# Shorter lag of the state sums, another order in the norm stage and in the first feed-forward tiles

## Chip, cores and metric

The kernel runs on one core of a Trainium2 chip. Time is device microseconds of one execution; the figure that counts is the median of several executions, lower is better.

## What is computed

One decoder layer over x (4 rows of the batch, 512 tokens, 512 wide) and a context ctx (4, 512, 256), all float32: attention, a selective scan gated by x, and a feed-forward part whose weights are drawn from a table of 16 values, each behind a residual and a layer norm.

```python
x = _layernorm(x + attn(x, weight_qkv, weight_proj))
x = _layernorm(x + ssm(ctx_1024, x, ...))      # x is the gate z
x = _layernorm(x + ffn(x, lut, gate_idx, up_idx, down_idx))

# ssm, per batch row: 512 channels, 16 states, 512 steps
x = einsum('ed,bld->bel', in_proj_w, ctx); u = silu(conv(x) + conv_b)
dt_lo, Bm, Cm = split(einsum('ke,bel->bkl', x_proj_w, u))
delta = softplus(einsum('er,brl->bel', dt_proj_w, dt_lo) + dt_proj_b)
state = state * exp(delta_t * A) + (delta_t * u_t) * B_t      # every step t
y = sum_n(state * C_t) + D * u
return y * silu(z)

# ffn
h = silu(x @ lut[gate_idx].T) * (x @ lut[up_idx].T)           # 1376 wide
return h @ lut[down_idx].T
```

## The kernel before

Each engine has a program of its own, written out by hand; its order is the order of the code, and semaphores tie the engines together. Nothing reorders it.

**Ramp (up to about 57 us).** SP loads in order: the table, the weights ip, ctx, xT (four loads), the first chunk of index words, wqkv. VectorE does the convolution's taps (`earlier_taps`, L1125), and behind the first and the second set the two integer operations on the index words (L1336, L1339). ScalarE makes u (`silu_u`, L822). TensorE does the kv projections (L563), which need xT and wqkv, and then the x projection (L577), which needs u.

**Scans (57 to 541 us).** The scan runs in 64 groups g (16 states for each of 4 batch rows), each of ET = 4 units et of 128 channels by 512 steps: 256 units k. For every unit TensorE transposes the scaled input into one of NB = 4 PSUM banks (`input_transposed`, L665), once the scan of unit k - 4 has freed the bank; VectorE scans it (`scan`, L1224); Pool multiplies the state by C (`output_product`, L1524). In the last batch row VectorE does the product of et = 3 itself (L1217, L1221). The states of the groups below G0 = 56 are added up in DRAM by accumulating DMAs of Pool's queue, even and odd groups apart. Those of groups 56 to 63 are added up on TensorE in PSUM (`state_summed`, L677): one pass per unit through the identity, two instructions of the trace. A sum waits for its unit's product and stands behind the input transpose of the unit 12 later. `rest_summed` (L683) adds what the DMAs have summed up for the last row.

**Norm stage (541 to about 612 us).** Batch rows b = 0 to 3, halves k = 0 to 7 (k = 2b and 2b + 1, two tiles of 128 tokens each). ScalarE makes the gates (`gates`, L999, L1000), those of row 3 once x1 of row 3 is loaded into hT, and then the high part of the first weights (`high_part`, L1046). VectorE multiplies y by the gate (`gate_y`, L1272, for row 3 L1269 out of PSUM); TensorE transposes the product (`y_over`, L715); VectorE adds x1 and takes the statistics (`norm_stats`, L1282 to L1292); Pool raises to -1/2 (`stage2_rstd`, L1614); VectorE makes the shift (`norm_shift`, L1297); ScalarE applies both (`norm_apply`, L1006); TensorE transposes (`x2_over`, L727); ScalarE writes the rounded high part (`x2T_hi`, L1017), VectorE the remainder (`x2T_lo`, L1306). TensorE does, for k = 0 to 7, x2_over(k), y_over(k + 3), and from k = 3 on halves of the first gate/up product between them. y_over(4) waits for gate_y(3), which frees its banks, and for its own row's gate_y(2). Pool's order is stage2_rstd(0) to (3), `low_part(0, 0)` (L1629, the remainder of the first weights), stage2_rstd(4) and on.

**Feed-forward (612 to 849 us, then the down product).** Weights are decoded in chunks, gate_up(f) and down(f), from one byte per entry: ScalarE makes 7 leaves (`leaves`, L1036), Pool the eighth (L1624), and VectorE joins them in 7 selects (`select`, L1252), each waiting for certain leaves. After select 2 and 3 VectorE spreads the bits of the next chunk (`then`, L1231, L1236). SECOND is the chunk gate_up 1, decoded while the norm stage runs; WITH_HALF says behind which half ScalarE makes which of its leaves. TensorE does `gate_up(f)` in four blocks tb (L743, 24 matmuls each); ScalarE's `silus` (L1052) and VectorE's `inner` (L1313) turn a block into hT. TensorE's block tb of tile f + 1 waits for inner(f, tb), and all of it for the low part of its weights. In `tile(f)` the decodes of down f and gate_up f + 2 are mixed with the silus and inners; tile(0) stands ahead of the loop over f.

## Time and profile before

| | us |
|---|---|
| median of 3 runs | 983.32 (982.26 to 984.1) |
| profiled execution | 979.72 |
| its span, first to last instruction | 977.9 |

| engine | busy us | share |
|---|---|---|
| TensorE matmul | 843.4 | 86% |
| VectorE | 779.3 | 80% |
| ScalarE | 668.1 | 68% |
| Pool (GpSimd) | 480.1 | 49% |

The mean granted clock of TensorE is 0.918 of full speed. The shares are means over stages with different limits; each stage has to be read for itself. Of an engine's idle time the trace names what ended it. Idle time of an engine that others do not wait for costs nothing.

### The profile page before, as it was taken

To read this page: it belongs to the slowest core of one execution; us is meant where nothing else is said; L and a number is where in the kernel's file an instruction comes from. 1 tells how busy PE (TensorE), PEld (TensorE's weight loads), DVE (VectorE), ACT (ScalarE), POOL (GpSimd) and SP (SyncE) were. 2 spreads that over 40 slices of the span, in tenths; PEclk is the share of its full clock that TensorE was granted. 3 is DMA by queue.
4 is the path that set the end of the run, shared out by engine and by line. 5 is a ranking of instruction groups with operands and counts; after the bars stand their busy time and mean duration, and the time that the engine had idled before them with its cause. 6 is when DMAs were issued, how large, how long until landed. Compare 5 with 4: busy or idle time off the path is not lost.

```text
span 977.9 us, 11750 instructions
## 1 busy us (share of the span) xinstructions
PE 843.4 (86%) x3736; PEld 609.0 (62%) x3736; DVE 779.3 (80%) x1084; ACT 668.1 (68%) x989; POOL 480.1 (49%) x456
## 2 busy tenths in 40 slices
PE   7879897878779697887879858799999999899996
PEld 3547644557445574546555457687777778688885
DVE  5997899887998969987699897888888887355543
ACT  4598995689966899658689346777777776242321
POOL 3169966799866999569877231211121111001000
PEclk9899878989789897798879979899999999999999
DMA  8057988689996799967999722111111110223221
GB/s 289 35 158 177 216 181 211 118 227 238 220 218 137 200 224 223 226 136 171 219 228 306 196 78 100 52 44 43 43 45 62 43 43 22 75 86 108 86 65 54
DMA packets 50340, 137.04 MB, mean 140 GB/s; under 512 B 5540, under 2 KB 13860, under 8 KB 41588
## 3 DMA queue, kind: packets, MB, share of 16 engines
q0 software_dynamic: 8064, 58.72, 31.6%
q1 hardware_dynamic: 40864, 77.49, 23.3%
q8 instruction: 23, 0.38, 0.2%
q10 hardware_dynamic: 1364, 0.25, 0.1%
q14 instruction: 25, 0.20, 0.1%
HBM read 58.46 MB, written 79.04 MB: 141 GB/s over the span
## 4 chain that ended last, share of the span: by engine, by line
issue 21%; PE 18%; DVE 15%; ACT 9%; POOL 5%; DMA 1%; DVEq 1%; ACTq 0%; POOLq 0%
PE banks L768 4%; PE banks L627 4%; DVE leaf L1252 3%; PE banks L743 3%; ACT leaf L1036 2%; DVE w_gu L1252 2%; PE banks L677 2%; POOL state L1524 2%; DVE state L1224 2%; PE banks L665 2%; ACT decay L921 2%; ACT scaled L908 2%; DMA y_scratch<-state 1%; DVE idx_sb L1236 1%; DVE w_down L1252 1%
## 5 line engine op out<-in xcount | busy, mean ns | idle before, releaser
L1524 POOL TENSOR_TENSOR state<-state,crep 128x512 f32<-128x512 f32 x243 | 333.4, 1600 | 80.5 <-DVE state L1224 80.4
L1224 DVE TENSOR_TENSOR_SCAN state<-decay,banks 128x512 f32<-128x512 f32 x243 | 280.8, 1203 | 54.8 <-PE banks L665 44.9
L743 PE MATMUL banks<-x2T,wgu 128*128 128x512 f32 x1056 | 250.1, 396 | 10.0 <-DVE hT L1313 5.4
L665 PE MATMUL banks<-ident,scaled 128*128 128x128 f32 x1024 | 171.1, 308 | 77.0 <-DVE state L1224 56.6
L743 PEld LDWEIGHTS banks<-x2T,wgu 128*128 128x128 f32 x1056 | 199.3, 190 | 58.8 <-DVE hT L1313 13.3
L665 PEld LDWEIGHTS banks<-ident,scaled 128*128 128x128 f32 x1024 | 132.4, 157 | 149.6 <-DVE state L1224 65.5
L921 ACT ACTIVATE decay<-delta,negA 128x512 f32<-128x512 f32 x256 | 170.4, 730 | 75.1 <-DVE state L1224 66.9
L908 ACT ACTIVATE scaled<-duT,BT 128x512 f32<-128x512 f32 x256 | 164.4, 728 | 0.3 <-issue 0.3
L1036 ACT ACTIVATE leaf<-idx_sb,table,table_gap 128x512 f32<-128x512 uint8 (+1 forms) x126 | 122.5, 1014 | 7.1 <-DVE w_down L1252 3.1
L1623 POOL TENSOR_TENSOR pool_wait_here<-minus_half 128x1 f32<-128x1 f32 x21 | 5.2, 246 | 181.7 <-DVE w_gu L1252 116.8
L1252 DVE COPY_PREDICATED leaf<-idx_sb,leaf 128x512 f32<-128x512 uint8 (+1 forms) x84 | 89.0, 1060 | 5.9 <-issue 4.9
L768 PE MATMUL banks<-x2T 128*128 128x512 f32 (+1 forms) x264 | 83.1, 396 | 3.5 <-DVE x2T L1461 3.5
L768 PE MATMUL banks<-x2T,wgu 128*128 128x512 f32 (+1 forms) x264 | 81.5, 390 | 0.0
L1659 POOL TENSOR_TENSOR rstd<-vareps,minus_half 128x1 f32<-128x1 f32 x16 | 8.7, 544 | 140.7 <-DVE vareps L1480 140.7
L627 PE MATMUL banks<-wp,attT 128*128 128x512 f32 x128 | 64.0, 647 | 0.0
L768 PEld LDWEIGHTS banks<-x2T 128*128 128x128 f32 (+1 forms) x264 | 50.6, 192 | 14.7 <-issue 3.9
L1537 POOL DMA_DIRECT2D y_scratch<-state x52 | 56.1, 1079 | 2.4 <-DMA y_scratch<-state 2.4
L768 PEld LDWEIGHTS banks<-x2T,wgu 128*128 128x128 f32 (+1 forms) x264 | 49.6, 188 | 10.4
L1113 ACT ACTIVATE leaf<-leaf,shift,rstd 128x512 f32<-128x512 f32 x16 | 13.1, 817 | 62.6 <-DVE shift L1483 62.6
L1252 DVE COPY_PREDICATED w_gu<-idx_sb,leaf 128x1024 f32<-128x1024 uint8 x30 | 48.5, 1618 | 0.1
L569 PE MATMUL banks<-wqkv,xT_sb 128*128 128x512 f32 x96 | 44.7, 610 | 1.5 <-DVE conv_in L1181 1.5
L1046 ACT ACTIVATE wgu<-w_gu 128x1024 fp32r<-128x1024 f32 x11 | 11.7, 1060 | 50.1 <-DVE w_gu L1252 50.1
(152 smaller groups left out, 1164.4 us busy)
## 6 DMA issues: line engine op xcount, KB each, us to landing
y_scratch<-state POOLq DMA_DIRECT2D x52, 1024.0 KB, 8.9
crep<-c_scratch SPq DMA_DIRECT2D x64, 256.0 KB, 5.8
idx_sb<-in_idx SPq DMA_DIRECT2D x10, 512.0 KB, 3.6
xT_sb<-in_xT SPq DMA_DIRECT2D x16, 256.0 KB, 5.0
y_scratch<-u SPq DMA_DIRECT2D x4, 1024.0 KB, 7.0
y_scratch<-state SPq DMA_DIRECT2D x4, 1024.0 KB, 6.3
leaf<-x_scratch SPq DMA_DIRECT2D x16, 256.0 KB, 2.8
out<-leaf SPq DMA_DIRECT2D x16, 256.0 KB, 2.1
```

Of the source, the lines that this page charges most:

```text
L569: last = mm(banks[:, bank, :], xT_sb[:, t, s, :], wqkv[:, t, 0:QT * P], start=t == 0, stop=t == HT - 1)
L627: last = mm(banks[:, bank, :], attT[:, s, t if s else 0, :], wp[:, t, :], start=t == 0, stop=t == QT - 1)
L665: last = nc.tensor.transpose(banks[:, k % NB, lc * LQ:(lc + 1) * LQ], scaled[:, g % SR, lc, et * P:(et + 1) * P], ident[:])
L743: last = mm(banks[:, 2 * tb + w, :], wgu[par][:, w, ws, t * P:(t + 1) * P], x2T[:, tb, xs, t, :], start=t == 0 and n == 0, stop=t == HT - ...
L768: last = mm(banks[:, bank, :], h[0:rows], w[0:rows, f, :], start=f == 0 and n == 0, stop=f == FT - 1 and n == 2)
L908: A(scaled[:, g % SR, lc, :], duT[m % 2][:, lc, :], ACT.Copy, scale=BT[:, m % 2, lc, n:n + 1])\
L921: A(decay[:, k % DR_RING, :], delta[m % 2][:, et, :], ACT.Exp, scale=negA[:, et, n:n + 1])\
L1036: A(buffer(LEAF_ROLE[j], kind, parity), bit_of(0, kind, parity), ACT.Identity, bias=table[:, 2 * j:2 * j + 1], scale=table_gap[:, j:j + 1] ...
L1224: V.tensor_tensor_scan(state[:, g % GR, et, :], decay[:, k % DR_RING, :], banks[:, k % NB, :], 0.0, ALU.mult, ALU.add).then_inc(scan_ready, 1)
L1252: V.copy_predicated(buffer(kept, kind, parity), bit_of(bit, kind, parity), buffer(other, kind, parity)).then_inc(mux_ready, 1)
L1524: G.tensor_tensor(state[:, g % GR, et, :], state[:, g % GR, et, :], crep[:, g % CR, :], ALU.mult)\
L1537: pool.dma_start(total[:, b], group(g), accum_op=ALU.add).then_inc(group_sum(g)[0], 16)
```

## The change

1. SP loads the first index words ahead of xT, behind ctx.
2. The state sums stand behind the input transpose of the unit 7 later (SUM_LAG), not 12.
3. VectorE: the order becomes gate_y(0), norm_stats(0), gate_y(1), norm_stats(1), norm_shift(0), gate_y(2), norm_stats(2), and norm_shift(2) goes ahead of `second_gap`. GATED, the count of gate_y instructions after which a row is gated, follows. Pool does low_part(0, 0) behind stage2_rstd(2).
4. ScalarE makes leaf 4 of SECOND behind half 6; VectorE does select 2 of SECOND ahead of x2T_lo(6).
5. In tile(0), not in the loop, silus and inners of blocks 2 and 3 go ahead of the decode of gate_up 2.

```diff
+        SUM_LAG = 7
-        GATED = {0: 1, 1: 2, 3: 6, 2: 7}
+        GATED = {0: 1, 1: 2, 2: 3, 3: 7}
...
                 load_ctx(0)
+                sp.dma_start(first_words, idx[0, :, 0:2 * H]).then_inc(first_idx_in, 16)
                 load_xT(0)
-                sp.dma_start(first_words, idx[0, :, 0:2 * H]).then_inc(first_idx_in, 16)
...
-                    if k // ET - 3 >= G0:
-                        state_summed(k // ET - 3, k % ET)
-                for g in range(DS * S - 3, DS * S):
-                    for et in range(ET):
-                        state_summed(g, et)
+                    if k - SUM_LAG >= ET * G0:
+                        state_summed(*divmod(k - SUM_LAG, ET))
+                for k in range(UNITS - SUM_LAG, UNITS):
+                    state_summed(*divmod(k, ET))
...
-                WITH_HALF = {2: (0,), 3: (1,), 4: (2,), 5: (3,)}
+                WITH_HALF = {2: (0,), 3: (1,), 4: (2,), 5: (3,), 6: (4,)}
...
-                leaves(*SECOND, (4, 5, 6))
+                leaves(*SECOND, (5, 6))
...
                         silus(f, 0)
+                    if isinstance(f, int):
+                        silus(f, 2)
+                        silus(f, 3)
                     leaves("gate_up", f + 2, early)
...
-                    silus(f, 2)
-                    silus(f, 3)
+                    if not isinstance(f, int):
+                        silus(f, 2)
+                        silus(f, 3)
...
                 gate_y(0)
+                norm_stats(0)
                 gate_y(1)
-                norm_stats(0)
                 norm_stats(1)
                 norm_shift(0)
+                gate_y(2)
                 norm_stats(2)
                 norm_shift(1)
                 x2T_lo(0)
                 gate_y(3)
                 norm_stats(3)
+                norm_shift(2)
                 second_gap()
-                gate_y(2)
-                norm_shift(2)
...
+                select(*SECOND, (2,), then=("down", 0))
                 x2T_lo(6)
-                select(*SECOND, (2, 3), then=("down", 0))
+                select(*SECOND, (3,), then=("down", 0))
...
                     select("down", f, then=("gate_up", f + 2))
-                    if not isinstance(f, int):
+                    if isinstance(f, int):
+                        inner(f, 2)
+                        inner(f, 3)
+                    else:
                         inner(f, 0)
...
-                for k in range(4):
+                for k in range(3):
                     stage2_rstd(k)
                 low_part(0, 0)
-                for k in range(4, 7):
+                for k in range(3, 7):
                     stage2_rstd(k)
```

TensorE at the end of the scans, before: an input transpose (L665) and a state sum (L677) in turns, then the sums that are left, then y_over(0) (L715).

```order
247 L677 MATMUL banks<-state,ident 128x512
248 L665 MATMUL banks<-ident,scaled 128x128 x4
249 L677 MATMUL banks<-state,ident 128x512
250 L665 MATMUL banks<-ident,scaled 128x128 x4
251 L677 MATMUL banks<-state,ident 128x512 x13
252 L715 MATMUL banks<-ident,rows_in 128x128 x8
```

The same place after (the lines are L666, L678 and L715 there).

```order
257 L678 MATMUL banks<-state,ident 128x512
258 L666 MATMUL banks<-ident,scaled 128x128 x4
259 L678 MATMUL banks<-state,ident 128x512
260 L666 MATMUL banks<-ident,scaled 128x128 x4
261 L678 MATMUL banks<-state,ident 128x512 x8
262 L715 MATMUL banks<-ident,rows_in 128x128 x8
```

Behind the last input transpose stand 8 sums, not 13; the five others stand in the scans.

VectorE in the norm stage, before: gate_y(3) is L1269, gate_y(2) the L1272 from hT, norm_shift L1297.

```order
313 L1306 TENSOR_TENSOR x2T<-banks,x2T 128x2x256 x2
314 L1269 TENSOR_TENSOR hT<-banks,hT 128x512 x4
315 L1282 TENSOR_TENSOR rows_in<-banks,rows_in 128x512
316 L1282 TENSOR_TENSOR rows_in<-banks,conv_in 128x512
317 L1286 BN_STATS stats<-rows_in 128x6 x2
318 L1289 BN_AGGR meanvar<-stats 128x2 x2
319 L1292 TENSOR_SCALAR vareps<-meanvar 128x2
320 L1395 TENSOR_TENSOR table_gap<-table 128x8
321 L1397 TENSOR_SCALAR table_gap<-table_gap 128x8
322 L1272 TENSOR_TENSOR rows_in<-rows_in,hT 128x2048
323 L1297 SCALAR_TENSOR_TENSOR shift<-meanvar,rstd 128x2
324 L1306 TENSOR_TENSOR x2T<-banks,x2T 128x2x256 x2
```

The same place after (lines 4 higher), from gate_y(2) to x2T_lo(0), and on to x2T_lo(1).

```order
309 L1276 TENSOR_TENSOR rows_in<-rows_in,hT 128x2048
310 L1286 TENSOR_TENSOR rows_in<-banks,rows_in 128x512 x2
311 L1290 BN_STATS stats<-rows_in 128x6 x2
312 L1293 BN_AGGR meanvar<-stats 128x2 x2
313 L1296 TENSOR_SCALAR vareps<-meanvar 128x2
314 L1301 SCALAR_TENSOR_TENSOR shift<-meanvar,rstd 128x2
315 L1310 TENSOR_TENSOR x2T<-banks,x2T 128x2x256 x2
316 L1273 TENSOR_TENSOR hT<-banks,hT 128x512 x4
...
321 L1296 TENSOR_SCALAR vareps<-meanvar 128x2
322 L1301 SCALAR_TENSOR_TENSOR shift<-meanvar,rstd 128x2
323 L1399 TENSOR_TENSOR table_gap<-table 128x8
324 L1401 TENSOR_SCALAR table_gap<-table_gap 128x8
```

gate_y(2) has gone from behind norm_stats(3) to ahead of norm_stats(2), and norm_shift(2) follows norm_stats(3) at once.

## Rows read from the trace of the kernel before

**Rows 1.** Windows by stage: length; busy PE, PEld, DVE, ACT, POOL; clock, DMA.

```profile
541.50:612.50 71.00, 53.42 (x248) 40.59 (x246) 57.46 (x111) 35.80 (x49) 14.51 (x14) 0.88 0.36 117
612.50:823.00 210.50, 203.90 (x864) 163.25 (x864) 184.81 (x338) 151.51 (x175) 43.98 (x48) 0.98 0.15 44
```

**Rows 2.** Timeline, VectorE, ramp: start, length, instruction, [idle before it <- releaser].

```profile
13.58 0.69 DVE L1336 TENSOR_SCALAR scaled<-scaled 128x1024 int32<-128x1024 int32 x1 [1.01 <-DMA scaled<-in_idx]
```

**Rows 3.** Timeline, SP's queue and TensorE, ramp.

```profile
5.61 1.81 SPq L453 DMA_DIRECT2D scaled<-in_idx  x1
...
17.57 3.69 PE L563 MATMUL banks<-wqkv,xT_sb 128*128 128x256 f32 x16 [3.10 <-DMA wqkv<-in_wqkvT]
22.36 3.60 PE L577 MATMUL banks<-u,xp_w 128*48 128x512 f32 x8 [1.10 <-ACT u L822]
```

**Rows 4.** Timeline, VectorE, last scans.

```profile
515.40 3.44 DVE L1224 TENSOR_TENSOR_SCAN state<-decay,banks 128x512 f32<-128x512 f32 x3 [3.18 <-DMA y_scratch<-state]
...
540.77 0.69 DVE L1221 TENSOR_TENSOR state<-banks,crep 128x512 f32<-128x512 f32 x1
```

**Rows 5.** Timeline, TensorE, end of the scans.

```profile
536.38 0.60 PE L665 MATMUL banks<-ident,scaled 128*128 128x128 f32 x4
536.82 11.32 PE L677 MATMUL banks<-state,ident 128*128 128x512 f32 x26
```

**Rows 6.** Timeline, Pool, the last products.

```profile
537.55 3.73 POOL L1524 TENSOR_TENSOR state<-state,crep 128x512 f32<-128x512 f32 x3 [0.26 <-DVE state L1224]
```

**Rows 7.** Timeline, VectorE, norm stage.

```profile
545.35 2.29 DVE L1272 TENSOR_TENSOR rows_in<-rows_in,gate_in 128x2048 f32<-128x2048 f32 x1 [1.69 <-DMA rows_in<-y_scratch]
548.72 1.29 DVE L1282 TENSOR_TENSOR rows_in<-banks,rows_in 128x512 f32<-128x512 f32 x2 [1.07 <-PE banks L715]
...
559.02 1.29 DVE L1306 TENSOR_TENSOR x2T<-banks,x2T 128x512 fp32r<-128x512 f32 x2 [0.18 <-ACT x2T L1017]
560.23 2.47 DVE L1269 TENSOR_TENSOR hT<-banks,hT 128x512 f32<-128x512 f32 x4
...
565.72 2.28 DVE L1272 TENSOR_TENSOR rows_in<-rows_in,hT 128x2048 f32<-128x2048 f32 x1
567.92 2.30 DVE L1297 SCALAR_TENSOR_TENSOR shift<-meanvar,rstd 128x2 f32<-128x2 f32 x1
```

**Rows 8.** Timeline, ScalarE, norm stage.

```profile
551.92 1.49 ACT L999 ACTIVATE hT<-hT 128x1536 f32<-128x1536 f32 x1 [12.81 <-DMA hT<-x_scratch]
...
553.83 1.04 ACT L1046 ACTIVATE wgu<-w_gu 128x1024 fp32r<-128x1024 f32 x1
556.00 1.52 ACT L1006 ACTIVATE rows_in<-rows_in,shift,rstd 128x512 f32<-128x512 f32 x2 [1.12 <-DVE shift L1297]
...
570.26 1.52 ACT L1006 ACTIVATE rows_in<-rows_in,shift,rstd 128x512 f32<-128x512 f32 x2 [7.17 <-DVE shift L1297]
```

**Rows 9.** One line, Pool's low parts: ns min/median/max, first and last start.

```profile
L1629 POOL TENSOR_TENSOR wgu<-w_gu,wgu x11: 2348/2405/3955, 566.2 to 813.9; 128x1024 fp32r<-128x1024 f32 x11
```

**Rows 10.** Window 566 to 569 (columns of rows 1), then TensorE's timeline.

```profile
566.00:569.00 3.00, 0.86 (x4) 0.89 (x5) 3.00 (x2) 0.00 (x0) 3.00 (x2) 0.50 0.00 0
...
568.14 1.94 PE L715 MATMUL banks<-ident,rows_in 128*128 128x128 f32 x8 [5.71 <-DVE rows_in L1272]
```

**Rows 11.** Timeline, ScalarE and VectorE, second chunk: leaves and select 3.

```profile
598.63 3.51 ACT L1036 ACTIVATE leaf<-idx_sb,table,table_gap 128x1024 f32<-128x1024 uint8 x3
...
601.04 1.40 DVE L1252 COPY_PREDICATED leaf<-idx_sb,leaf 128x1024 f32<-128x1024 uint8 x1 [3.42 <-issue]
```

**Rows 12.** Timeline, first tile: ScalarE, VectorE, TensorE.

```profile
616.51 1.25 ACT L1036 ACTIVATE w_gu<-idx_sb,table,table_gap 128x1024 f32<-128x1024 uint8 x1 [0.99 <-DVE idx_sb L1236]
...
621.21 1.59 DVE L1252 COPY_PREDICATED leaf<-idx_sb,leaf 128x1024 f32<-128x1024 uint8 x1 [0.86 <-issue]
...
629.51 57.15 PE L743 MATMUL banks<-x2T,wgu 128*128 128x512 f32 x240 [4.05 <-DVE hT L1313]
```

**Rows 13.** Timeline, TensorE, a tile in the loop (one of five such rows).

```profile
686.89 22.51 PE L743 MATMUL banks<-x2T,wgu 128*128 128x512 f32 x96 [0.23 <-DVE hT L1313]
```

More of the change, by code:

```diff
@@ L1442, in tile @@
                     select("gate_up", f + 2, range(3, 6), then=("down", f + 1))
-                    inner(f, 2)
+                    if not isinstance(f, int):
+                        inner(f, 2)
                     select("gate_up", f + 2, (6,))
-                    inner(f, 3)
+                    if not isinstance(f, int):
+                        inner(f, 3)
                 tile(0)
```

## Prediction, made before the changed kernel ran

> **What bounds the kernel now.** I read the windows by stage first, then the order of each engine at the places that the edits touch. In the norm stage (541.5 to 612.5 us) no engine is full: VectorE is busy 57.5 of 71.0 us, TensorE 53.4, ScalarE 35.8; it is a chain of short steps handed from engine to engine, and idle time there costs what it lasts if it lies on the chain. In the first feed-forward stage (612.5 to 823) TensorE is busy 203.9 of 210.5 us and looks like the bound [rows 1], but each tile of it begins with 0.23 us of waiting for an hT product of VectorE [rows 13]. VectorE in turn waits for ScalarE's leaves: the tables are decoded by those two in turns, and TensorE arrives first. So that stage ends when the decoding ends, and what counts for an edit ahead of it is how much sooner the last select of the second chunk is done. I go through the program in order and carry the gain to that point. Times below are on the profiled run's own clock.
>
> **1. The first index words are loaded ahead of xT.** Before, the load is issued at 5.61 us, behind the four xT loads [rows 3], and VectorE, done with its taps, stands 1.01 us until it has landed [rows 2]. Issued some 3.4 us sooner it lands before VectorE asks, so the wait goes. Who is late next: the kv projections start at 17.57 when wqkv lands; since SP's queue issues the same bytes ahead of wqkv in either order, I leave that at 17.57. They take 3.69 us, to 21.26; the x projection begins at 22.36 after waiting 1.10 us for u, the end of VectorE's taps [rows 3]. Cover under the gain is thus 1.10 us, the gain 1.01. xT comes later, by about one 512 KB load, but is first read with wqkv. From there to the first scan VectorE, ScalarE and TensorE follow one chain, which moves as a whole. Bounds: 0 (if the load, now right behind ctx, slows ctx down by as much) to 1.1. I take **1.0**.
>
> **2. The state sums trail by 7 units, not 12.** After the last input transpose (536.38) TensorE runs 26 passes in 11.32 us [rows 5], that is 13 sums of 0.87 us, and is free at 548.0. Now 8 sums are left. The first four are ready at 536.9; the next three need Pool's products, the three of 3.73 us from 537.55 [rows 6], which end near 538.8, 540.0 and 541.3; the last needs VectorE's product, ended at 541.5 [rows 4]. TensorE takes them one behind the other without waiting: 536.9 + 8 x 0.87 = 543.8. It is free 4.2 us sooner. In the scans a sum now stands three units behind the scan that released TensorE. Twenty units take 26.1 us, 515.40 to 541.46 [rows 4], 1.30 each, so that is 3.9 us; Pool begins its first product as the scan ends (0.26 us idle), takes 1.25 us for each where a scan takes 1.15 [rows 4, 6], and its third is done some 1.5 us behind the scan: no wait of its own.
>
> **3. The norm stage.** Of the 4.2 us only part is usable, for two reasons.
> VectorE now does gate_y(0), to 543.7; the sums of x1 and y may start 0.7 us behind TensorE's release, at 544.5, not 548.72 [rows 7]. A set of norm_stats takes 2.8 us: from gate_y(3) at 560.23, 2.4 us, to 565.72 are 5.5 us, less 0.3 for the table gap. A gate_y of rows 0 to 2 takes 2.2 (565.72 to 567.92) [rows 7]. So 544.5 + 2.8 (stats 0) + 2.2 (gate 1; its row landed at 545.35 [rows 7]) + 2.8 + 0.1 + 2.2 (gate 2) + 2.8 + 0.1 = 557.5, when VectorE is ready for x2T_lo(0). Before, that began at 559.02 with gate_y(2) still to do.
> ScalarE however waits 12.81 us for the last x1 rows, which land at 551.92, then does gates(3) and the high part, to 554.87, and began norm_apply(0) at 556.00 [rows 8]. With its shift ready at 552.4 it can start at 554.87 and no sooner. From its start to x2T_lo(0) are 3.0 us (556.00 to 559.02): 557.9. That is later than VectorE's 557.5, so ScalarE sets it, and the gain here is 559.02 - 557.9 = 1.1.
> Then x2T_lo(0), gate_y(3) and stats(3) as before, to 564.3 (565.72 less the table gap's 0.3, less 1.1). There gate_y(2), 2.2 us, no longer follows; and norm_shift(2), a 128x2 operation, no longer takes the 2.30 us [rows 7] that it took while Pool's low part ran, from 566.25 for 3.96 us where its other ten take 2.4 [rows 9], but 0.1. x2T_lo(1) starts at 570.2 - 1.1 - 2.2 - 2.2 = 564.7. The next norm_apply, which waited 7.17 us for that shift [rows 8], moves with it, and so do y_over(4), which waited for gate_y(2) [rows 10], and all that follows: **5.5**.
> The low part is moved to where VectorE does x2T_lo(0) and gate_y(3), 558.3 to 560.7. Each has one operand in PSUM, and the scans do too: beside Pool's 1.25 us products they keep their pace [rows 4, 6]. I cost the move at nothing; its cover is that kind of operand. If it stretched a VectorE operation as it did norm_shift(2), up to 2.2 us would come back.
> By the Trainium skill, "SBUF — State Buffer", section "SBUF: two separate sides", a VectorE operation with two SBUF inputs and a Pool operation exclude each other for the whole instruction, whichever starts first. The 3.96 us and the 2.30 us agree. The rule also speaks against the new order: Pool's rstd(0) and rstd(1) now come due just as gate_y(1) and gate_y(2), with two SBUF inputs, start, and would wait out 2.2 us each. Their shifts are not wanted for 2.8 us more, so by the rule the sum stays 6.6; without it norm_shift(2)'s 2.2 us would have another cause and might stay, sum 4.4.
> Against the 5.5 stands the clock. TensorE, finished 4.2 us sooner but held by a ScalarE that comes only 1.1 sooner, idles some 3 us longer ahead of x2_over(0). At the half clock that it has at 566 to 569, a group of 8 transposes takes 1.94 us [rows 10], at the full one half of that. If x2_over(0) falls to the half clock, x2T_lo(0) is 0.8 later. I take off 0.5: the norm stage gives **5.0**, between 2.8 (with the low part's stretch) and 5.5.
>
> **4. The second chunk's fifth leaf and third select are taken earlier.** VectorE stood 3.42 us before the select at 601.04, which waits for the second of three leaves that ScalarE runs from 598.63 in 3.51 us [rows 11]. One of the three now goes ahead of norm_apply(7). It delays that by 1.15 us, of which TensorE's gate/up half hides some 0.45; the waited leaf then ends at 598.63 + 0.7 + 1.15 = 600.5 for 600.97. x2T_lo(7) and the last select follow: **0.4**, bounds -0.5 and 1.2 (the whole leaf). The select taken ahead of x2T_lo(6) lies in VectorE's idle time.
>
> **5. The first tile is closed sooner.** TensorE waited 4.05 us at 629.51 for inner(0, 2) [rows 12], and that wait goes: silus and inners now stand ahead of the gate_up decode. But TensorE's next tile waits for inner(1, 0), on the decode's chain, so TensorE only comes there earlier and waits there. For the decode, two 0.6 us products move ahead of its selects, where 0.86 us of VectorE's waiting for a leaf [rows 12] takes part of them up, and one no longer stands before the last select. ScalarE's two silus fit in the 0.99 us in which it waited for the bits [rows 12]. I take **0.2**, bounds -0.6 and 0.9.
>
> Sum: 1.0 + 5.0 + 0.4 + 0.2 = **6.6 us**. The profiled execution, 979.72 us with a span of 977.9, would go to 973.1; the median of the runs shown is 3.6 above it, and 983.32 - 6.6 = **976.7**.
>
> **Rivals.**
> (a) *The clock takes back half.* The longer idle lets TensorE's half clock fall on x2_over(0), x2_over(3) and the first gate/up half too: 0.8 each for the two groups of 8, and up to 2 us on 12 matmuls of the wide kind. Gain 3.5, time **979.8**. For it: this stage is the one where the clock already was 0.50 [rows 10]. Against: most of what follows was at half clock already. The Trainium skill, "TensorE: Matmul & The Clock Gate", section "HAM oscillation", says that waits between bursts bring the slow clock back and the next burst starts cold; by that rule this case holds.
> (b) *TensorE is the feed-forward bound after all.* Then the removed 4.05 us counts in full: 983.32 - 6.4 - 4.05 = **972.9**. Against it the 0.23 us at every tile [rows 13].
> (c) *Slower: the sums clog TensorE's queue.* A sum waits in order for Pool's product, and the input transposes behind it feed the scans. With a sum a unit costs TensorE 0.44 + 0.87 = 1.3 us at full clock, just VectorE's pace; at half clock 2.6. Five more units now carry one. VectorE has three filled banks, 3.9 us, and ahead of 515.40 it waits 3.18 us for a sum's DMA anyway [rows 4], so a half-clock stretch there is free. Beyond 3 of the last 16 units at half clock each costs 1.3 us, and from 8 on the kernel is slower than before (8 x 1.3 - 3.9 = 6.5); with ten the loss is 13 - 3.9 = 9.1 and the time 983.32 - 6.6 + 9.1 = **985.8**. For it: TensorE has no slack there. Against: a busy TensorE kept its clock in that stretch.
> (d) *Nothing of it is measurable*: the scans' own scatter, or ctx landing later in the ramp and a later x1 landing in the norm stage, undo all but edits 4 and 5: 983.32 - 0.6 = **982.7**.
>
> **How the numbers follow.** Forecast 976.7: 0.63 (own range 974.5 to 978.9). (a) 979.8: 0.17. (b) 972.9: 0.07. (c) 985.8: 0.05. (d) 982.7: 0.08. The range takes in (a) and reaches down to (b) until 0.2 is out: 973.0 to 980.6. A measurement here tells some 0.2% (2 us) from no change. Faster by more: forecast, (a) and (b), with a little of (a) passing over: 0.86. Within it: (d) and that rest, 0.09. Slower: (c), 0.05.
>
> **What would show it.** Right: no VectorE idle before the first index operation and scans 1.0 us sooner; TensorE free of sums some 2.4 us after the last scan's product, not 6.5; norm_apply(0) right behind the high part; norm_shift(2) at 0.15 us and the low part at 2.4; the last select of the second chunk about 6.4 us earlier; TensorE's 4.05 us gone but an idle stretch of like size before its next tile; the same 22.51 + 0.23 us per tile. Wrong: a TensorE wait on Pool inside the last scans, a low part over 3 us, tiles shorter than 22.7 us.

## Result, and the profile of the changed kernel

The changed kernel ran in 976.34 us (median of 4 runs, 975.52 to 979.58) beside 982.79 us for the kernel before (981.49 to 984.1, 4 runs). The ratio is 0.9945, with a 95% interval of 0.9922 to 0.9969: a small gain, 5.4 us (3.0 to 7.7), but clear of no change. The forecast was 976.7, in a range of 973.0 to 980.6.

The profiled execution of the changed kernel is its slowest, 979.58 us with a span of 977.8, and that of before had a span of 977.9: the two profiles are equally long and yet differ at every place that the edits touch. So each is read in stretches, from a fixed event to a fixed event. I use three: up to the first scan, the scans (to the end of VectorE's last product, L1225, "scans' end"), and the **stage** from the scans' end to the start of the second chunk's last select. From there to the end is 369.9 to 370.3 us in every profile of this study.

Windows of before, then of after: length; busy PE, PEld, DVE, ACT, POOL; clock, DMA.

```profile
57.00:541.50 484.50, 395.13 (x1856) 261.89 (x1855) 420.22 (x444) 398.40 (x651) 399.73 (x359) 0.87 0.87 206
541.50:607.60 66.10, 51.29 (x240) 39.15 (x239) 55.10 (x107) 32.34 (x44) 11.24 (x11) 0.87 0.37 118
```

```profile
545.10:607.70 62.60, 47.82 (x228) 38.02 (x227) 52.86 (x109) 32.41 (x44) 13.70 (x11) 0.81 0.38 125
607.70:818.00 210.30, 200.78 (x855) 161.40 (x854) 182.84 (x331) 152.74 (x176) 45.87 (x48) 0.98 0.15 46
```

The stage went from 66.14 to 62.59 us, 3.55 less, at a lower clock (0.81 for 0.87). The scans' end stands at 545.08 for 541.46, 3.62 later: 0.16 of that is there at the first scan (57.30 for 57.14), the rest grew inside the scans. The first feed-forward stage [rows 1] is as long as before.

The ramp of after: SP's queue, TensorE, VectorE.

```profile
2.17 0.47 SPq L453 DMA_DIRECT2D scaled<-in_idx  x1
7.99 7.11 PE L555 MATMUL banks<-ctx_sb,ip 128*128 128x512 f32 x16 [0.48 <-DMA ctx_sb<-in_ctxT]
17.59 3.69 PE L564 MATMUL banks<-wqkv,xT_sb 128*128 128x256 f32 x16 [2.49 <-DMA wqkv<-in_wqkvT]
21.89 3.60 PE L578 MATMUL banks<-u,xp_w 128*48 128x512 f32 x8 [0.61 <-ACT u L822]
13.12 0.68 DVE L1340 TENSOR_SCALAR scaled<-scaled 128x1024 int32<-128x1024 int32 x1
```

VectorE's wait of 1.01 us [rows 2] is gone and the x projection starts 0.47 sooner [rows 3], but its first input, ctx, is there only at 7.99 (7.36 before).

TensorE of after at the end of the scans:

```profile
540.43 7.03 PE L678 MATMUL banks<-state,ident 128*128 128x512 f32 x16
547.42 1.06 PE L715 MATMUL banks<-ident,rows_in 128*128 128x128 f32 x8
...
560.82 1.97 PE L727 MATMUL banks<-ident,rows_in 128*128 128x128 f32 x8 [5.27 <-ACT rows_in L1006]
```

It is free of sums 2.38 us after the scans' end, not 6.68 [rows 5]. Behind y_over(2) it waits 5.27 us, and x2_over(0), 1.97 us for 1.13 before, runs at the half clock.

VectorE of after, from norm_stats(0) to x2T_lo(1):

```profile
548.53 1.29 DVE L1286 TENSOR_TENSOR rows_in<-banks,rows_in 128x512 f32<-128x512 f32 x2 [1.26 <-PE banks L715]
551.35 2.29 DVE L1276 TENSOR_TENSOR rows_in<-rows_in,gate_in 128x2048 f32<-128x2048 f32 x1
556.43 2.29 DVE L1276 TENSOR_TENSOR rows_in<-rows_in,hT 128x2048 f32<-128x2048 f32 x1
561.43 0.15 DVE L1301 SCALAR_TENSOR_TENSOR shift<-meanvar,rstd 128x2 f32<-128x2 f32 x1
562.73 1.42 DVE L1310 TENSOR_TENSOR x2T<-banks,x2T 128x512 fp32r<-128x512 f32 x2 [1.15 <-ACT x2T L1017]
...
569.26 0.15 DVE L1301 SCALAR_TENSOR_TENSOR shift<-meanvar,rstd 128x2 f32<-128x2 f32 x1
569.60 1.28 DVE L1310 TENSOR_TENSOR x2T<-banks,x2T 128x512 fp32r<-128x512 f32 x2
```

ScalarE, then Pool, in the same stretch:

```profile
556.41 1.48 ACT L999 ACTIVATE hT<-hT 128x1536 f32<-128x1536 f32 x1 [13.69 <-DMA hT<-x_scratch]
...
558.32 1.04 ACT L1046 ACTIVATE wgu<-w_gu 128x1024 fp32r<-128x1024 f32 x1
559.27 1.50 ACT L1006 ACTIVATE rows_in<-rows_in,shift,rstd 128x512 f32<-128x512 f32 x2
```

```profile
551.52 2.70 POOL L1624 TENSOR_TENSOR rstd<-vareps,minus_half 128x2 f32<-128x2 f32 x1 [6.62 <-DVE vareps L1296]
556.53 2.74 POOL L1624 TENSOR_TENSOR rstd<-vareps,minus_half 128x2 f32<-128x2 f32 x1 [2.31 <-DVE vareps L1296]
...
562.26 2.37 POOL L1639 TENSOR_TENSOR wgu<-w_gu,wgu 128x1024 fp32r<-128x1024 f32 x1
```

norm_apply(0) stands right behind the high part, with no wait of its own. ScalarE sets it, since the last x1 rows land only at 556.41. norm_shift(2) takes 0.15 us, not 2.30 [rows 7], and the low part 2.37, not 3.96 [rows 9]. Pool's rstd(0) and rstd(1), 0.70 where nothing runs against them, are held for 2.7 us beside gate_y(1) and gate_y(2).

The end of the stage on VectorE, and TensorE's second tile:

```profile
601.11 1.40 DVE L1256 COPY_PREDICATED leaf<-idx_sb,leaf 128x1024 f32<-128x1024 uint8 x1 [3.89 <-issue]
...
607.67 1.38 DVE L1256 COPY_PREDICATED w_gu<-idx_sb,leaf 128x1024 f32<-128x1024 uint8 x1
...
641.35 24.04 PE L743 MATMUL banks<-x2T,wgu 128*128 128x512 f32 x98 [4.98 <-DVE hT L1317]
```

TensorE's wait of 4.05 us for inner(0, 2) [rows 12] is gone, but TensorE waits 4.98 us ahead of the next tile (the last row runs on to the end of the view, so its count is not that of a tile).

### The profile page after: what moved, and what is told of

It reads as the page before. It is cut to its first block, busy times and chain, and to the rows that moved or that the text cites. A ratio compares the mean times of both kernels' runs of the same rounds, so it can differ in the third digit from the quotient of the medians.

```text
span 977.8 us, 11751 instructions
## 1 busy us (share of the span) xinstructions
PE 850.6 (87%) x3736; PEld 615.3 (63%) x3736; DVE 776.8 (79%) x1084; ACT 667.6 (68%) x989; POOL 481.4 (49%) x456
## 4 chain that ended last, share of the span: by engine, by line
issue 18%; PE 12%; DVE 11%; ACT 6%; POOL 5%; DMA 3%; DVEq 1%; ACTq 0%; POOLq 0%; SPq 0%
PE banks L743 4%; PE banks L768 4%; POOL state L1534 3%; DVE leaf L1256 3%; DVE w_gu L1256 2%; ACT leaf L1036 2%; PE banks L628 2%; DMA hT<-x_scratch 2%; DMA y_scratch<-y_scratch 1%; DVE idx_sb L1240 1%; DVE w_down L1256 1%; ACT decay L921 1%; ACT scaled L908 1%; DVE state L1228 1%; POOL rstd L1669 1%
## 5 line engine op out<-in xcount | busy, mean ns | idle before, releaser
L743 PEld LDWEIGHTS banks<-x2T,wgu 128*128 128x128 f32 x1056 | 199.8, 191 | 57.3 <-DVE hT L1317 13.0
L666 PE MATMUL banks<-ident,scaled 128*128 128x128 f32 x1024 | 171.6, 310 | 71.6 <-DVE state L1228 47.9
L666 PEld LDWEIGHTS banks<-ident,scaled 128*128 128x128 f32 x1024 | 134.3, 159 | 144.4 <-DVE state L1228 59.3
L570 PE MATMUL banks<-wqkv,xT_sb 128*128 128x512 f32 x96 | 49.9, 670 | 1.1 <-DVE conv_in L1185 1.0
```

Source lines behind the costliest of these rows:

```text
L570: last = mm(banks[:, bank, :], xT_sb[:, t, s, :], wqkv[:, t, 0:QT * P], start=t == 0, stop=t == HT - 1)
L666: last = nc.tensor.transpose(banks[:, k % NB, lc * LQ:(lc + 1) * LQ], scaled[:, g % SR, lc, et * P:(et + 1) * P], ident[:])
L743: last = mm(banks[:, 2 * tb + w, :], wgu[par][:, w, ws, t * P:(t + 1) * P], x2T[:, tb, xs, t, :], start=t == 0 and n == 0, stop=t == HT - ...
```

## Experiments

**Theory.** The gain is made in the norm stage, and edits 2 and 3 make it together: the sums are done sooner, and VectorE has an order that can use it. What ScalarE, the landing of x1 and TensorE's clock allow limits it. Edits 1, 4 and 5 add under 1.7 us. **Rivals.** One edit carries the gain alone; the low part's place does (Pool, not VectorE's order); the ramp does; the first tile does, if TensorE is the bound there.

All readings stand in this table, in us; the last four times count from the scans' end. "Ratio" is to the kernel before, with its 95% interval.

| kernel | ratio | ctx matmuls start | first scan | scans' end | norm_stats(0) | x2T_lo(0) | x2T_lo(1) | stage |
|---|---|---|---|---|---|---|---|---|
| before | 1 | 7.36 | 57.14 | 541.46 | 7.26 | 17.56 | 28.69 | 66.14 |
| after | 0.9945 [0.9922, 0.9969] | 7.99 | 57.30 | 545.08 | 3.45 | 17.65 | 24.52 | 62.59 |
| again | 0.9953 [0.9933, 0.9973] | 8.58 | 58.48 | 544.10 | 4.88 | 17.85 | 24.59 | 62.32 |
| u_lag | 0.9979 [0.9965, 0.9993] | 8.54 | 57.80 | 545.34 | 7.61 | 20.57 | 27.31 | 64.15 |
| u_norm | 0.9989 [0.9974, 1.0005] | 8.33 | 57.85 | 542.20 | 6.58 | 17.35 | 28.60 | 66.51 |
| p_apply | 0.9943 [0.9922, 0.9965] | 8.18 | 58.41 | 543.20 | 3.46 | 16.84 | 23.71 | 60.62 |
| u_low | 0.9955 [0.9933, 0.9976] | 8.18 | 56.98 | 541.58 | 3.46 | 16.80 | 23.67 | 62.59 |
| u_leaf | 0.9964 [0.9951, 0.9977] | 8.08 | 58.12 | 543.21 | 3.46 | 17.67 | 24.54 | 62.75 |
| u_tile | 0.9966 [0.9951, 0.9982] | 8.53 | 58.45 | 543.57 | 4.86 | 17.84 | 24.57 | 62.50 |
| u_ramp | 0.9961 [0.9944, 0.9978] | 7.53 | 57.37 | 541.97 | 4.88 | 18.44 | 25.17 | 62.54 |
| best | 0.9964 [0.9941, 0.9987] | 7.59 | 57.83 | 542.55 | 4.88 | 17.85 | 24.59 | 62.41 |
| best_warm | 0.9947 [0.9926, 0.9968] | 7.29 | 57.11 | 540.78 | 3.46 | 16.43 | 23.17 | 60.31 |
| p_mid | 0.9945 [0.9923, 0.9966] | 7.72 | 56.70 | 540.98 | 4.88 | 17.85 | 24.59 | 62.58 |
| p_warm | one run, 977.03 us | 7.88 | 58.00 | 543.25 | 3.46 | 16.69 | 23.43 | 61.77 |

From first scan to scans' end the profiles scatter from 483.67 to 487.78 us; the two kernels with the sums 12 behind (before 484.32, u_lag 487.54) stand at both ends of it. That scatter is as large as the whole gain, so the stage time of a profile separates single edits better than the runs do. The stage scatters too, in two things that differ already between two profiles of one and the same kernel, after and again. The last x1 rows land 10.46 to 11.46 us after the scans' end (11.33 and 10.84 in these two). And in the 15 us from x2T_lo(1) on, TensorE's granted clock is between 0.53 and 0.77 (0.55 and 0.66), behind that 1.00 up to the last select:

| clock in these 15 us | kernels | x2T_lo(1) to the last select, us |
|---|---|---|
| 0.75 to 0.77 | u_lag, p_apply, best_warm | 36.84 to 37.14 |
| 0.66 to 0.71 | before, again, u_leaf, u_ramp | 37.37 to 38.21 |
| 0.53 to 0.56 | the other seven | 37.82 to 38.92 |

So an edit whose work is done by x2T_lo(1) is read best at x2T_lo(1), and a difference of about 1 us in the whole stage can be that clock.

**again**: the changed kernel itself, as the base of the others.

> The changed kernel as it is, as the reference for the runs beside it. Time 976.3 us. M is the time from the end of VectorE's last product of the scans to the start of the last select of the second chunk: 66.1 us in the profile of before (541.46 to 607.60), 62.6 in the profile of after (545.08 to 607.67). Expected again 62.6, within 0.6, and the scans' end anywhere between 541 and 545, since it moved by 3.6 us between the two profiles with hardly an edit ahead of it.

The stage was 62.32, the ratio 0.9953. That is the same gain, of 4.6 us (2.7 to 6.6).

**u_lag**: edit 2 undone.

```diff
-        SUM_LAG = 7
+        SUM_LAG = 12
```

> The changed kernel with the state sums 12 units behind again. Theory: the sums end some 4.2 us later, VectorE's first statistics start as much later, VectorE is then the last to be ready for x2T_lo(0) (it had 1.15 us to spare in the profile of after), so M grows by 4.2 - 1.15 = 3.1, to 65.7, time 979.4. Rival (ScalarE and the x1 load set the norm stage, the sums are hidden): M stays 62.6, time 976.3.

TensorE's row of sums, VectorE's first norm_stats and ScalarE's norm_apply(0):

```profile
540.70 11.32 PE L678 MATMUL banks<-state,ident 128*128 128x512 f32 x26
...
552.95 1.29 DVE L1286 TENSOR_TENSOR rows_in<-banks,rows_in 128x512 f32<-128x512 f32 x2 [5.41 <-PE banks L715]
...
560.96 1.52 ACT L1006 ACTIVATE rows_in<-rows_in,shift,rstd 128x512 f32<-128x512 f32 x2 [1.66 <-DVE shift L1301]
```

The sums take their 11.32 us again and VectorE stands 5.41 us for them. x2T_lo(0) is 2.9 later than in after (3.1 was expected) and x2T_lo(1) 2.8, but the stage is 64.15, only 1.6 to 1.8 longer, where 3.1 was expected: the stretch behind x2T_lo(1) was 0.9 to 1.2 shorter than in again and after, at the higher clock of the table above (0.75 for 0.66 and 0.55). Of before's stage 2.0 us are gone even so, and the ratio, 0.9979, says the same (2.1 us).

**u_norm**: edit 3 undone, order of VectorE, GATED and Pool's low part.

```diff
-        GATED = {0: 1, 1: 2, 2: 3, 3: 7}
+        GATED = {0: 1, 1: 2, 3: 6, 2: 7}
...
-                norm_stats(0)
                 gate_y(1)
+                norm_stats(0)
...
-                gate_y(2)
...
-                norm_shift(2)
                 second_gap()
+                gate_y(2)
+                norm_shift(2)
...
-                for k in range(3):
+                for k in range(4):
```

> The changed kernel with the norm stage's order on VectorE and Pool as before (gate_y(1) ahead of norm_stats(0), gate_y(2) and norm_shift(2) behind norm_stats(3), low part behind rstd(3)), sums 7 behind. Theory: the order is worth gate_y(2)'s 2.2 us and the 2.2 us that norm_shift(2) waits for the low part: M 67.0, time 980.7, about where the kernel before is. Rival (the sums alone bring it): M within 1 of 62.6, time 977.3 or less.

VectorE: the second gate_y, then the late gate_y(2) and norm_shift(2); and Pool's low part.

```profile
546.57 2.29 DVE L1276 TENSOR_TENSOR rows_in<-rows_in,gate_in 128x2048 f32<-128x2048 f32 x1 [2.18 <-DMA rows_in<-y_scratch]
...
566.38 2.28 DVE L1276 TENSOR_TENSOR rows_in<-rows_in,hT 128x2048 f32<-128x2048 f32 x1
568.58 2.30 DVE L1301 SCALAR_TENSOR_TENSOR shift<-meanvar,rstd 128x2 f32<-128x2 f32 x1
```

```profile
566.91 3.96 POOL L1639 TENSOR_TENSOR wgu<-w_gu,wgu 128x1024 fp32r<-128x1024 f32 x1
```

TensorE had the sums done 2.38 us after the scans' end, and it brought nothing: VectorE's next instruction was gate_y(1), whose row from DRAM was not there for 2.18 us, and norm_stats(0) came at 6.58 for 7.26. The stage is 66.51, no shorter than before's 66.14, and the time 0.9989, not told apart from no change. By the stage the sums alone are worth 0, the order alone 2.0, both 3.6 to 3.8 (each with edit 4 in it). At x2T_lo(1), ahead of the stretch that the clock stretches or shortens, it is clearer still: 28.69 before, 28.60 with the sums alone, 27.31 with the order alone, 24.52 and 24.59 with both, so 0.1, 1.4 and 4.1 to 4.2 us. The theory holds: neither edit carries the gain alone.

**p_apply**: the change with norm_apply(0) ahead of the high part on ScalarE.

```diff
-                high_part(0, 0)
...
+                high_part(0, 0)
```

> The changed kernel with ScalarE's norm_apply(0) ahead of the high part of the first weights. Theory (ScalarE, waiting for the last x1 rows, is the chain to x2T_lo(0)): norm_apply(0) starts right behind gates(3), 0.97 us sooner; VectorE waits 1.15 us there, so x2T_lo(0) and M come 0.9 to 1.0 sooner, M 61.6, time 975.3. Rival (the gate/up half and its clock set the stage further on): M within 0.3 of 62.6.

ScalarE, then TensorE:

```profile
556.57 1.50 ACT L1006 ACTIVATE rows_in<-rows_in,shift,rstd 128x512 f32<-128x512 f32 x2
557.98 1.04 ACT L1046 ACTIVATE wgu<-w_gu 128x1024 fp32r<-128x1024 f32 x1
```

```profile
558.13 1.97 PE L727 MATMUL banks<-ident,rows_in 128*128 128x128 f32 x8 [4.45 <-ACT rows_in L1006]
```

norm_apply(0) comes 0.8 sooner, x2T_lo(0) too (16.84 for 17.65), though x1 landed 0.13 later than in after (11.46 for 11.33), so that ScalarE set x2T_lo(0) is shown. The stage, 60.62, fell by 2.0, where 1.0 was expected; the time, 0.9943, can't be told from the change's own. Where the rest of the 2.0 comes from is seen with best, below.

**u_low**: only Pool's low part back behind stage2_rstd(3).

```diff
-                for k in range(3):
+                for k in range(4):
```

> The changed kernel with Pool's low part behind rstd(3) again, VectorE's order as changed. Theory (a Pool operation shuts out VectorE operations that read only SBUF): the low part now starts when rstd(3) is done, about when x2T_lo(1) (PSUM) runs, and holds up the integer operation on the index words behind it, 0.6 us long, until it ends: that one shows up to 2.4 us, M grows by 1.0 to 1.8. Rival (only two SBUF inputs are shut out): the integer operation keeps 0.68 us, M 62.6. Second rival (moving the low part was what took away the 2.30 us of norm_shift(2), whatever runs beside it): norm_shift(2) is long again; against that, it now comes before rstd(3) ends.

VectorE, then Pool:

```profile
565.25 1.28 DVE L1310 TENSOR_TENSOR x2T<-banks,x2T 128x512 fp32r<-128x512 f32 x2
566.44 2.20 DVE L1235 TENSOR_SCALAR idx_sb<-idx_sb 128x1024 int32<-128x1024 int32 x1
```

```profile
565.73 2.37 POOL L1639 TENSOR_TENSOR wgu<-w_gu,wgu 128x1024 fp32r<-128x1024 f32 x1
```

norm_shift(2), now ahead of it, stays at 0.15 and the low part at 2.37: it was VectorE's order that freed both, not Pool's. In its old place the low part holds up the integer operation behind x2T_lo(1), 2.20 us for the 0.68 it takes in after. The stage is 62.59 where 1.0 to 1.8 more was expected, but x2T_lo(1) came 0.85 sooner, since x1 landed at 10.48 here. From x2T_lo(1) to the last select are 38.92 us, the longest of all kernels (36.8 to 38.3 in the others), and TensorE waits 0.76 us, at 569.39, for the statistics' product behind the held operation, a wait that after doesn't have. So the stretch probably costs near 1 us, and Pool's move is worth that at most; one profile doesn't settle it.

**u_leaf**: edit 4 undone. **u_tile**: edit 5 undone.

```diff
-                WITH_HALF = {2: (0,), 3: (1,), 4: (2,), 5: (3,), 6: (4,)}
+                WITH_HALF = {2: (0,), 3: (1,), 4: (2,), 5: (3,)}
...
-                select(*SECOND, (2,), then=("down", 0))
                 x2T_lo(6)
-                select(*SECOND, (3,), then=("down", 0))
+                select(*SECOND, (2, 3), then=("down", 0))
```

> The changed kernel with leaf 4 behind norm_apply(7) and select 2 behind x2T_lo(6), as before. Theory of the prediction: select 3 starts 0.4 us later against the end of the scans, M 63.0, time 976.7. Rival, from the profile of after, where TensorE waited 0.58 us for the later norm_apply(7): leaf 5 ends at the same time either way, M 62.6, and the first gate/up blocks 2 and 3 start 0.5 sooner.

```diff
-                    if isinstance(f, int):
-                        silus(f, 2)
-                        silus(f, 3)
                     leaves("gate_up", f + 2, early)
...
-                    if not isinstance(f, int):
-                        silus(f, 2)
-                        silus(f, 3)
+                    silus(f, 2)
+                    silus(f, 3)
```

> The changed kernel with the first tile as before. Theory: TensorE's wait for inner(0, 2), 4 us, comes back at the third block and the one of 4.98 us ahead of the next tile goes; the decode's chain is as it was: from the first select of down 0 to the first select of down 1 are 22.0 us in the profile of after (611.59 to 633.57) and 21.9 in that of before, so it stays within 0.2, time 976.3. Rival (b) of the prediction: 4 us slower, 980.4.

In u_leaf, norm_apply(7) starts at 593.42 and the waited select at 599.40, 5.98 us; in after the leaf that now stands ahead of norm_apply(7) starts at 595.46 and the select at 601.11, 5.65 us. Edit 4 gives 0.33 at its place; the stage (62.75 for 62.32 and 62.59) doesn't contradict it, but can't show it either. TensorE of u_tile (the row runs on to the end of the view):

```profile
627.97 32.23 PE L743 MATMUL banks<-x2T,wgu 128*128 128x512 f32 x131 [4.04 <-DVE hT L1313]
```

The wait is back, and nothing is lost: from the first down select to the next, once around the first tile, are 21.85 us with edit 5 undone and 21.89 before, 21.97 to 22.04 in the twelve kernels with it. The decode sets the tile, and edit 5 costs 0.1 rather than gives 0.2.

**u_ramp**: edit 1 undone. **p_mid**: the words behind the second of the four xT loads (with p_apply's edit).

```diff
-                sp.dma_start(first_words, idx[0, :, 0:2 * H]).then_inc(first_idx_in, 16)
                 load_xT(0)
+                sp.dma_start(first_words, idx[0, :, 0:2 * H]).then_inc(first_idx_in, 16)
```

> The changed kernel with the first index words loaded behind xT. In the profile of after ctx landed 0.63 us later than before and VectorE's wait of 1.01 us for the words was gone; the selects of the ramp started 0.47 us sooner. Theory: the edit is worth those 0.5 us at most up to there, and the start of the first scan moves with TensorE's clock by as much; time 976.8. Rival (the 1.0 us of the prediction): 977.3, selects 1.0 us later against after.

```diff
+                        if c == 0 and t == 1:
+                            sp.dma_start(first_words, idx[0, :, 0:2 * H]).then_inc(first_idx_in, 16)
...
-                sp.dma_start(first_words, idx[0, :, 0:2 * H]).then_inc(first_idx_in, 16)
                 load_xT(0)
```

> norm_apply(0) ahead of the high part, and the first index words loaded behind the second of the four xT loads. Theory (the words slow ctx down only when they follow it at once): ctx lands by 7.6 us, the words land before VectorE's first taps end, VectorE's 1.0 us of waiting goes and the ramp's selects start at 20.7. Rival (any place ahead of the last xT load is as late as behind it, since the bytes ahead are what counts, or ctx is slowed as well): selects at 21.2 or later.

TensorE and VectorE of u_ramp, of again, and of p_mid:

```profile
7.53 7.11 PE L555 MATMUL banks<-ctx_sb,ip 128*128 128x512 f32 x16 [0.25 <-DMA ctx_sb<-in_ctxT]
13.74 0.69 DVE L1340 TENSOR_SCALAR scaled<-scaled 128x1024 int32<-128x1024 int32 x1 [1.00 <-DMA scaled<-in_idx]
```

```profile
8.58 7.11 PE L555 MATMUL banks<-ctx_sb,ip 128*128 128x512 f32 x16 [1.86 <-DMA ctx_sb<-in_ctxT]
17.60 5.38 PE L564 MATMUL banks<-wqkv,xT_sb 128*128 128x256 f32 x16 [1.92 <-DMA wqkv<-in_wqkvT]
```

```profile
7.72 7.10 PE L556 MATMUL banks<-ctx_sb,ip 128*128 128x512 f32 x16 [0.64 <-DMA ctx_sb<-in_ctxT]
12.84 0.68 DVE L1341 TENSOR_SCALAR scaled<-scaled 128x1024 int32<-128x1024 int32 x1
```

With the words right behind it, ctx is there at 7.88 to 8.58 us (nine kernels, after among them); with them behind xT at 7.29 to 7.59 (before and three); with two xT loads between, at 7.72. In u_ramp VectorE's wait is back, and the first scan still stands at 57.37. The first scan comes at 57.9 on average of the nine with the words ahead (56.98 to 58.48) and at 57.36 of the four without: edit 1 wins 1.0 us of waiting, gives as much up at ctx, and may lose some 0.5 more. In four of the nine the kv projections ran in part at the half clock, 5.38 us for 3.69 (and 5.12 in one of the four without). p_mid has both, no wait and an early ctx. Its x projection starts at 21.62 (22.36 before, 21.89 in after), and its first scan, 56.70, is the earliest of all, though by only 0.3 and in one profile. The time, 0.9945, can't be told from the change's.

**p_warm**: 20 transposes of ident into an unread bank behind y_over(2), to keep TensorE busy (each is two passes in the rows). **best**: p_apply with edit 1 undone. **best_warm**: both, with 16 such transposes.

```diff
                 y_over(2)
+                for _ in range(20):
+                    mm(banks[:, 3, 0:P], ident[:], ident[:], start=True, stop=True)
```

> The changed kernel with 20 small matmuls of the identity with itself (4.4 us at full clock) between y_over(2) and x2_over(0), ScalarE as changed. In the profile of after TensorE idles 5.27 us there, x2_over(0) takes 1.97 us, x2T_lo(0) starts 17.65 us behind the scans' end. Theory (that idle brings the half clock on x2_over(0)): 1.1 us for x2_over(0), x2T_lo(0) at 16.8 to 16.9, M 61.8. Rival: unchanged.

> The changed kernel with ScalarE's norm_apply(0) ahead of the high part and the first index words behind xT again. Theory from the profiles so far: with the words ahead of xT ctx lands 0.6 to 1.2 us later and the first scan starts at 56.98 to 58.48, mean 57.9 of 8 profiles; with them behind at 57.14 and 57.37. So the edit of the ramp costs about 0.6 us; here the first scan starts at 57.3, M is 60.6 as with norm_apply(0) moved alone, and the time is some 0.6 us below that kernel: 975 to 976. Rival (the ramp's edit gains its 1.0 us): 0.5 to 1 us above it.

> The same, with 16 small matmuls of the identity with itself (3.5 us at full clock, results overwritten) ahead of x2_over(0), where TensorE idles. Theory (the idle brings the half clock on the transposes and the first gate/up half): the granted clock stays at 1.0 up to x2_over(0) and past it, x2_over(0) takes 1.1 us and not 2, M 59.8 to 60.2. Rival (the half clock comes from the gaps behind x2_over(0)): M 60.6, half clock from some 10 us later on.

TensorE of p_warm, and of best_warm:

```profile
553.57 4.63 PE L754 MATMUL banks<-ident 128*128 128x128 f32 x40
558.48 1.09 PE L727 MATMUL banks<-ident,rows_in 128*128 128x128 f32 x8 [0.29 <-ACT rows_in L1008]
```

```profile
551.09 3.74 PE L754 MATMUL banks<-ident 128*128 128x128 f32 x32
554.91 1.09 PE L727 MATMUL banks<-ident,rows_in 128*128 128x128 f32 x8
```

With TensorE kept busy up to it, x2_over(0) takes 1.09 us for 1.97. A wait alone doesn't decide it, though: behind waits of the same 2.57 us x2_over(0) took 1.13 before and 1.97 in best, and in u_ramp 1.10 behind 3.28.

```profile
557.57 1.13 PE L727 MATMUL banks<-ident,rows_in 128*128 128x128 f32 x8 [2.57 <-ACT rows_in L1006]
```

```profile
557.01 1.97 PE L727 MATMUL banks<-ident,rows_in 128*128 128x128 f32 x8 [2.57 <-ACT rows_in L1006]
```

In p_warm x2T_lo(0) is 1.0 sooner than in after; 0.5 of that is x1, which landed 10.81 us behind the scans' end for 11.33, and 0.4 the clock. The stage is 61.77, 0.8 shorter, all of it ahead of x2T_lo(1): from there on TensorE's clock fell to 0.53 all the same. best_warm, with p_apply's edit and a TensorE kept busy, has the shortest stage of all, 60.31.

In best, the expectation missed: the stage is 62.41, not 60.6, and the first scan stands at 57.83, not 57.3. Two things lie behind the stage. First, VectorE's norm_stats(0) in best, which waits for y_over(0):

```profile
547.43 1.29 DVE L1286 TENSOR_TENSOR rows_in<-banks,rows_in 128x512 f32<-128x512 f32 x2 [2.68 <-PE banks L715]
```

In five of the twelve kernels with a lag of 7 (again, u_tile, u_ramp, best, p_mid) TensorE had its last input transposes later against VectorE's scans and is free of sums 3.95 us after the scans' end, not 2.38. Then VectorE, 13.0 us of work behind norm_stats(0), is ready for x2T_lo(0) only at 17.85, in again, u_tile, best and p_mid alike (18.44 in u_ramp, where TensorE also waited 1.41 us for the load that `rest_summed` reads): VectorE sets it, not ScalarE, and norm_apply(0) at 12.89 in best gains nothing. Second, the clock. The 15 us from x2T_lo(1) on and the rest up to the last select, for after, then for p_apply:

```profile
569.60:584.60 15.00, 10.50 (x43) 9.47 (x44) 13.57 (x33) 8.94 (x12) 2.92 (x4) 0.55 0.19 71
584.60:607.67 23.07, 21.97 (x117) 18.14 (x116) 17.38 (x33) 15.18 (x21) 2.14 (x4) 1.00 0.24 92
```

```profile
566.91:581.91 15.00, 10.23 (x52) 9.46 (x53) 13.57 (x33) 9.05 (x13) 2.91 (x4) 0.77 0.18 70
581.91:603.82 21.91, 20.80 (x109) 17.12 (x107) 17.39 (x34) 15.06 (x21) 2.12 (x4) 1.00 0.26 97
```

In these 15 us TensorE has a clock of 0.55 in after, 0.77 in p_apply, and 0.56 in best: in the same time it gets through 43 instructions in after and 52 in p_apply. So of p_apply's 2.0 us, 0.8 are its order, and the other 1.2, all of it behind x2T_lo(1), go with the clock. That they are due to it is the likely reading, since over all fourteen profiles a higher clock there goes with a shorter stretch; no run sets the clock of this stretch by itself. By time no kernel here is clearly better than the change; best_warm and p_mid have the lowest medians (975.7 and 975.6 us).

## Why the prediction was right, point by point

The number was right, and its sum of 6.6 us was too large. The measured gain is 5.4 (3.0 to 7.7), and the ten kernels that keep edits 2 and 3 (after, again, and all others but u_lag, u_norm and p_warm) have a mean ratio of 0.9954, 4.5 us, and a mean stage of 62.1, 4.0 less than before. Four of the ten also have p_apply's edit; the six without it have 0.9957, 4.2 us, and a stage of 62.55, 3.6 less. I take the gain to be 4 to 5 us. The terms below add up to some 3.4 to 3.7, so that the median came out at 976.34, within 0.4 of the forecast, is in part luck: nothing but scatter is known for the rest.

- **Term 1, the ramp, 1.0: about 0.** The step that failed is the choice between its bounds. The lower one, 0 "if the load, now right behind ctx, slows ctx down", is what happens: it is there 0.5 to 1.2 us later than before. The cover of 1.10 us ahead of u was rightly seen, and p_mid, whose x projection starts 0.74 us sooner than before, suggests that most of the gain is there when ctx is left alone.
- **Term 2, the sums: right for after, not always.** TensorE is free 2.38 us after the scans' end (2.4 predicted), 4.3 sooner. In five of the other kernels it is 3.95, which the working, made from one phase of TensorE against VectorE, did not see. TensorE's waits on Pool's products in the last scans are 0.2 us in after and 0.5 in again, and the scans of the lag-7 kernels, 483.67 to 487.78 and 485.0 on average, can't be told from those at lag 12 (484.32 and 487.54); rival (c) did not occur.
- **Term 3, the norm stage, 5.0: 3.2 to 3.5.** Right in its mechanism: norm_apply(0) right behind the high part, gate_y(2) off the path between x2T_lo(0) and x2T_lo(1), norm_shift(2) at 0.15 us. x2T_lo(0) to x2T_lo(1) is 6.87 us for 11.13, 4.26 less where 4.4 was summed. What failed is the 1.1 ahead of x2T_lo(0), which was -0.1: x1 landed 11.33 us after the scans' end instead of 10.46 (0.8 later at norm_apply(0)), and x2_over(0) at the half clock put 0.4 more between that and x2T_lo(0) (3.46 for 3.02). The last 0.6 to 1.0 was lost behind x2T_lo(1), in whose first 15 us after had a clock of 0.55 and before 0.71. So the 0.5 set aside for the clock fits at x2_over(0) and was too little for the whole stage, and nothing was set aside for x1. The late x1 is scatter rather than an effect of the edits: u_low, with after's order on ScalarE and TensorE, has x1 at 10.48 and x2T_lo(0) at 16.80. The clock behind x2T_lo(1) scatters as well, so how much of its loss the edits cause stays open.
- **The low part's move, at nothing:** right for what it now stands beside. But that norm_shift(2)'s 2.30 us went is due to VectorE's order, not to this move (u_low).
- **Term 4, 0.4: 0.33** by its own rows, too little to be seen in the stage or the time.
- **Term 5, 0.2: -0.1.** Its argument held: TensorE's 4.05 us went, and it waited 4.98 for the next tile instead. Rival (b) is refuted by u_tile.
- **Rival (a)** names a mechanism that is in the rows of after: against before, x2_over(0) took 1.97 us for 1.13, x2_over(3) 1.97 for 1.39, the first gate/up half 4.01 for 3.64. That is 1.8 us of busy time where (a) had up to 3.6, and the missing gain of the ramp and the late x1 are no part of it. Its gain of 3.5 is nearer to 4 to 5 than the forecast's 6.6, in part by luck. By the Trainium skill, "TensorE: Matmul & The Clock Gate", section "HAM oscillation", a burst behind a wait starts cold; the trace agrees, 1.97 us behind 5.27 us of waiting, 1.09 behind filled time. Behind waits of 2.57 us it came out both ways, 1.13 before and 1.97 in best, so the wait alone doesn't settle it. But of the ten kernels with a lag of 7 and nothing to fill the wait, nine have x2_over(0) at 1.97 (u_ramp has 1.10); the two with a lag of 12 have 1.13 and 1.38. The rival had deserved more than 0.17.
- **Rival (d)** named the two things that did occur, ctx later in the ramp and x1 later in the norm stage; it was wrong in how much they undo, since x2T_lo(1) still came 4.2 us sooner.

## What to carry to other kernels

A gain on a chain of engines passes only if the next engine's order can use it: the sums 4.3 us sooner were worth 0.1 us at x2T_lo(1) with VectorE's old order and 2.8 with the new one (in the whole stage nothing, and 1.6 to 1.8). So price two such edits together, and test them by undoing each. Ahead of the first matmul of this kernel, a load put right behind the one that is waited for delayed it; with two 256 KB loads between the two most of that was gone (7.72 us, one profile). Where TensorE will be left waiting by the very edit that frees it, set aside something for the half clock on all bursts behind, not only on the next one: here it was 0.4 us at the first and about 1 us, up or down, behind it. Read stretches between fixed events when two profiles of equal span hide the difference.

## What the runs showed of the hardware that was not expected

- A load's neighbour behind it on SP's queue delays it: ctx's first matmul started at 7.88 to 8.58 us with the 512 KB of words right behind (nine kernels), 7.29 to 7.59 with them behind xT (four), 7.72 with two 256 KB loads between (one). That the two share the DMA engines is the likely cause and was not tested apart.
- Pool's 128x1024 product also holds up a VectorE operation with one input in SBUF: the int32 TENSOR_SCALAR took 2.20 us beside it (u_low), 0.68 alone. The x2T_lo and hT products, one operand in PSUM, kept their pace beside it. The Trainium skill, "SBUF — State Buffer", section "SBUF: two separate sides", names VectorE's two-port modes beside operations with two SBUF inputs; that fits if this one runs in such a mode, which the trace doesn't say.
- VectorE and Pool hold each other up in both directions: Pool's rstd took 2.70 and 2.74 us beside gate_y, 0.70 alone. The prediction had foreseen this, and that it costs nothing here: rstd(0) and rstd(1) ended 2.1 us before their shifts began.
- The same instructions of the same stage took 1.2 us more or less from x2T_lo(1) on, beside a clock of 0.55 or 0.77 over the first 15 us of it (after and p_apply). With TensorE kept busy up to x2_over(0) that clock was 0.53 in p_warm and 0.77 in best_warm.
- Kernels that differ only behind the scans ended them up to 3.5 us apart (541.58 in u_low, 545.08 in after).
